# Batching TensorE's matmuls by tile shape in one cross-attention of a twelve-sublayer network

## Chip, core and metric

The kernel runs on one NeuronCore of a Trainium2 chip. The metric is the device time of one execution in microseconds, as a median of runs. All data are fp32. The engines named below are TensorE (PE in the profile, with its weight loads as PEld), VectorE (DVE), ScalarE (ACT), GpSimd (POOL) and SyncE (SP), which issues the DMAs.

## The reference, cut to what matters

The network has four layers, each with a cross-attention, a self-attention-like sublayer and a feed-forward one, over x of shape (64, 32, 128). The change is in the second layer's cross-attention, the fourth of twelve sublayers that run one after the other:

```python
x = x + _L1_xattn_ref(_layernorm(x), ctx_1024, ctx_1024, Wq, bq, Wk, bk, Wv, bv, Wo, bo)
# 16 heads of 64, 64 batches, 32 queries, 257 keys, ctx of shape (64, 257, 128)
scores = einsum('bhqd,bhkd->bhqk', q, k) / sqrt(64)
probs = softmax(scores, axis=-1)
z = einsum('bhqk,bhkd->bhqd', probs, v)          # then z @ Wo + bo
```

## The kernel before

Every sublayer is a function that writes the instruction streams of the engines by hand, with semaphores between them, and ends with a barrier of all engines. `l1_xattn` first folds the weights: `wqk[h]` is Wq times Wk of head h, `wvo[h]` is Wv times Wo, so keys and values are the raw context. Then `strip_attention` (tiles with the prefix `l1xs_`) works through 16 groups of 4 batches. A group has 16 heads; a head of a group is one step t, 256 steps in all.

For one group TensorE does four kinds of work, and they use three tile shapes of its array:

- `project(g, r)`, r = 0 to 3 (L2332): the queries of 4 heads, 4 matmuls of the full 128 by 128 array, into the bank `m_ps`. VectorE's `take_queries` (L2419) adds the bias and stores them in `qx`.
- `score(g, n)`, n = 0 to 15 (L2345): 4 matmuls on tiles of 128 rows by 32 columns, one for each batch, into one bank of 257 columns; the keys move.
- `weigh(g, j)`, j = 0 to 8 (L2357): 4 matmuls on tiles of 32 rows by 128 columns, for one strip of 32 keys of each batch, 512 columns each, into the four banks `u_ps`. ScalarE's `take_u` (L2401) copies the four banks to `ub`.
- `merge(g, heads)` (L2369): 16 matmuls of the full array with `wvo`, summed in `m_ps` as well. VectorE's `result` (L2442) adds the sum to X.

An fp32 matmul shows as two MATMUL records in the trace, so a score, a weighing or a quarter projection is 8 records and a merge 32.

Between score and weighing a step passes through the softmax: `maximum` on VectorE (L2425), `exp` on ScalarE with the sum of the row (L2393), `inverse` on VectorE (L2430), a scaling on GpSimd (L2467, tile `p`), and `turn` on VectorE, a transpose in 32 by 32 blocks (L2437, tile `pt`). `p` and `col` have four buffers. The scores have three banks, `s_ps`, used in turn: score t waits for exp of t - 3.

The order on TensorE is written out: in iteration i, after score n of group i + 1, it does a half merge of group i - 1 (n = 0, 1), a weighing of group i (n in `weigh_at`) or a quarter projection of group i + 2 (n in `project_at`). So almost every score is followed by work of another shape. On VectorE the order is also written out: step t does the maximum of t, the inverse of t - 1 and the turn of t - 2. ScalarE puts the four copies of `take_u` behind the exps 13, 14 and 15 of the next group. SyncE loads keys and values of each group two groups ahead into double buffers.

Of the kernel before, what the change touches and what calls it, by code (L numbers as in the profile page):

```python
# [11 lines left out]
ALU = mybir.AluOpType  # L12
ACT = mybir.ActivationFunctionType
AX = mybir.AxisListType
# [4 lines left out]
S2 = 257  # L19
KC, NKC = 86, 3  # L20
SP2 = KC * NKC
H = 16
# [3 lines left out]
GROUPS, STRIP = B // 4, 9  # L26
# [2264 lines left out]
def strip_attention(k, nm, wqk, bqk, wvo, bo, ph):  # L2291

    nc = k.nc
    s = {n: k.sem(nm + n) for n in ("q_mm", "qx", "s_mm", "mx", "exp", "rec", "norm", "pt", "u_mm", "u", "o_mm", "x",
                                    "pad")}
# [10 lines left out]
    weigh_at, project_at = (2, 3, 4, 6, 7, 8, 10, 11, 12), (5, 9, 13, 15)  # L2306

    with nc.Block() as block:
        @block.sync
# [11 lines left out]
        @block.tensor  # L2321
        def _(pe):
            def project(g, r):

                if r > 0:
                    pe.wait_ge(s["qx"], 4 * g + r)
                elif g > 0:
                    pe.wait_ge(s["qx"], 4 * g)
                    if g >= 3:
                        pe.wait_ge(s["x"], g - 2)  # L2330
                for h in range(4):
                    mm = nc.tensor.matmul(m_ps[:, h * 128:(h + 1) * 128], wqk[:, 4 * r + h, :], k.XN[:, cols(g)],  # L2332
                                          start=True, stop=True)
                mm.then_inc(s["q_mm"], 1)

            def score(g, n):
                t = 16 * g + n
                if n == 0:
                    pe.wait_ge(keys_in[g % 2], (g // 2 + 1) * 16)
                if n % 4 == 0:  # L2340
                    pe.wait_ge(s["qx"], 4 * g + n // 4 + 1)
                if t >= 3:
                    pe.wait_ge(s["exp"], t - 2)
                for c in range(4):
                    mm = nc.tensor.matmul(s_ps[t % 3][32 * c:32 * c + 32, :S2], qx[:, g % 2, n, 32 * c:32 * c + 32],  # L2345
                                          keys[:, g % 2, c, :S2], start=True, stop=True)
                mm.then_inc(s["s_mm"], 1)

            def weigh(g, j):
                if j == 0:  # L2350
                    pe.wait_ge(s["pt"], 16 * g + 16)
                    pe.wait_ge(vals_in[g % 2], (g // 2 + 1) * 16)
                    if g > 0:
                        pe.wait_ge(s["u"], 4 * g)
                for c in range(4):
                    r = slice(32 * c, 32 * c + 32)
                    mm = nc.tensor.matmul(u_ps[c][:], vals[r, g % 2, j, :], pt[r, g % 2, :, j, :], start=(j == 0),  # L2357
                                          stop=(j == STRIP - 1))
                if j == STRIP - 1:
                    mm.then_inc(s["u_mm"], 1)  # L2360

            def merge(g, heads):
                if heads[0] == 0:
                    pe.wait_ge(s["u"], 4 * g + 4)
                    pe.wait_ge(s["qx"], 4 * min(g + 3, GROUPS))
                    if g > 0:
                        pe.wait_ge(s["x"], g)
                for h in heads:
                    mm = nc.tensor.matmul(m_ps[:, :128], wvo[:, h, :], ub[:, :, h, :], start=(h == 0), stop=(h == H - 1))  # L2369
                if heads[-1] == H - 1:  # L2370
                    mm.then_inc(s["o_mm"], 1)

            for r in range(4):
                project(0, r)
            for i in range(-1, GROUPS + 1):
                for n in range(16):
                    if i + 1 < GROUPS:
                        score(i + 1, n)
                    if n < 2 and i >= 1:
                        merge(i - 1, range(8 * n, 8 * n + 8))  # L2380
                    if n in weigh_at and 0 <= i < GROUPS:
                        weigh(i, weigh_at.index(n))
                    if n in project_at and i + 2 < GROUPS:
                        project(i + 2, project_at.index(n))

        @block.scalar
        def _(act):
            def exp(g, n):
                t = 16 * g + n
# [3 lines left out]
                nc.scalar.activation(p[:, t % 4, :S2], s_ps[t % 3][:, :S2], ACT.Exp, bias=col[:, 0, t % 4:t % 4 + 1],  # L2393
                                     accum_out=col[:, 1, t % 4:t % 4 + 1]).then_inc(s["exp"], 1)

            def take_u(g, c):
                if c == 0:
                    act.wait_ge(s["u_mm"], g + 1)
                    if g > 0:
                        act.wait_ge(s["o_mm"], g)  # L2400
                nc.scalar.copy(ub[:, c].rearrange("p h q -> p (h q)"), u_ps[c][:]).then_inc(s["u"], 1)  # L2401

            act.wait_ge(s["pad"], 1)
            for i in range(-1, GROUPS):
                for n in range(16):
                    if i + 1 < GROUPS:
                        exp(i + 1, n)
                    if n >= 13 and i >= 0:
                        take_u(i, n - 13)
                if i >= 0:  # L2410
                    take_u(i, 3)

        @block.vector
        def _(dve):
            def take_queries(g, r):
                dve.wait_ge(s["q_mm"], 4 * g + r + 1)
                if g >= 2:
                    dve.wait_ge(s["s_mm"], 16 * (g - 2) + 4 * r + 4)
                nc.vector.tensor_tensor(qx[:, g % 2, 4 * r:4 * r + 4, :], m_ps.rearrange("p (h t) -> p h t", h=4),  # L2419
                                        bqk[:, 4 * r:4 * r + 4].unsqueeze(2).to_broadcast([128, 4, 128]), ALU.add  # L2420
                                        ).then_inc(s["qx"], 1)

            def maximum(t):
                dve.wait_ge(s["s_mm"], t + 1)
                nc.vector.tensor_reduce(col[:, 0, t % 4:t % 4 + 1], s_ps[t % 3][:, :S2], AX.X, ALU.max, negate=True  # L2425
                                        ).then_inc(s["mx"], 1)
# [12 lines left out]
            def result(g):  # L2439
                dve.wait_ge(s["o_mm"], g + 1)  # L2440
                x = k.X[:, cols(g)]
                nc.vector.scalar_tensor_tensor(out=x, in0=m_ps[:, :128], scalar=bo, in1=x, op0=ALU.add, op1=ALU.add  # L2442
                                               ).then_inc(s["x"], 1)
# [4 lines left out]
            last = 16 * GROUPS  # L2448
            for t in range(last + 2):
                if t < last:  # L2450
                    maximum(t)
                if 1 <= t <= last:
                    inverse(t - 1)
                if t >= 2:
                    turn(t - 2)
                if t % 16 == 2 and t // 16 >= 2:
                    result(t // 16 - 2)
                if t % 16 in project_at and t // 16 + 1 < GROUPS:
                    take_queries(t // 16 + 1, project_at.index(t % 16))
            result(GROUPS - 2)  # L2460
            result(GROUPS - 1)

        @block.gpsimd
# [1255 lines left out]
```

## Time and profile before

| | us |
|---|---|
| median of 3 runs | 3266.33 (3265.39 to 3274.02) |
| profiled execution, first to last instruction | 3273.0 |
| steps of the cross-attention in it, first score to last result | 509 to 962 |
| one group in its steady part | 28.0 |

The profiled execution has no time of its own beside its span; the span lies inside the spread of the three runs, so what surrounds the instructions is not seen as a separate term. The span is read as the time of that execution. A window of the trace is given in microseconds from the start of the span. A row of the timeline gives start, duration, engine, line, operation, tiles, shape and count.

### The profile page before, as it was taken

What the parts mean: (1) busy time and instruction counts of PE and PEld (TensorE: products, weight loads), DVE (VectorE), ACT (ScalarE), POOL (GpSimd) and SP (SyncE); (2) the same over time, 40 slices, a digit from 0 to 9 for tenths busy, and PEclk for the clock granted to TensorE, in tenths of its full rate; (3) what the DMA queues carried; (4) which work ended last, traced back from release to release, by engine and by line L of the source; (5) the groups of instructions that cost most, each with busy time, mean ns of one, the idle gap of its engine ahead of it and who ended that gap; (6) DMA issues with size and microseconds to landing.
All of it is one profiled execution on the core that took longest, in us unless ns stands there. A gap on an engine that the chain in (4) does not pass through costs nothing. (4 is left out here: it accounts for less than half of the span.)

```text
span 3273.0 us, 114088 instructions
## 1 busy us (share of the span) xinstructions
PE 2717.9 (83%) x49115; PEld 1960.9 (60%) x49115; DVE 2148.9 (66%) x5489; ACT 1435.8 (44%) x3330; POOL 571.5 (17%) x592
## 2 busy tenths in 40 slices
PE   8987478999986788888888887679999998697745
PEld 5645365444445576676767676557776666386633
DVE  3348335555547988898888888267777665664741
ACT  4343233333343354444544454357776434363410
POOL 0000334555550000000000000000001332161024
PEclk9879688999997899999999898979999998898865
DMA  2100331111110000000000000001111001252013
GB/s 81 53 18 14 101 122 49 43 43 43 43 57 3 3 4 4 4 5 4 4 4 4 4 4 4 3 20 26 26 26 44 1 1 34 82 133 68 5 44 106
DMA packets 69907, 109.22 MB, mean 33 GB/s; under 512 B 10336, under 2 KB 55024, under 8 KB 68880
## 3 DMA queue, kind: packets, MB, share of 16 engines
q1 hardware_dynamic: 57776, 80.34, 8.0%
q0 software_dynamic: 11696, 22.40, 2.7%
q8 instruction: 357, 5.85, 0.7%
q14 instruction: 78, 0.64, 0.1%
HBM read 90.06 MB, written 16.51 MB: 33 GB/s over the span
## 5 line engine op out<-in xcount | busy, mean ns | idle before, releaser
L3087 PE MATMUL psum<-l1d_rw,l1d_cols 64*32 64x32 f32 (+2 forms) x20480 | 238.9, 215 | 86.4 <-issue 65.9
L3087 PEld LDWEIGHTS psum<-l1d_rw,l1d_cols 64*32 64x32 f32 x20480 | 208.9, 107 | 131.0 <-issue 104.9
L2467 POOL TENSOR_SCALAR l1xs_p<-l1xs_p,l1xs_col 128x257 f32<-128x257 f32 x256 | 237.9, 932 | 243.8 <-DVE l1xs_col L2430 243.3
L2393 ACT ACTIVATE l1xs_p<-psum,l1xs_col 128x257 f32<-128x257 f32 x256 | 122.1, 477 | 258.7 <-DVE l1xs_col L2425 257.9
L2425 DVE TENSOR_REDUCE l1xs_col<-psum 128x1 f32<-128x257 f32 x256 | 107.1, 418 | 155.9 <-PE psum L2345 155.8
L1747 POOL TENSOR_SCALAR X<-X,l1f_bias 128x512 f32<-128x512 f32 x4 | 6.3, 1584 | 1140.5 <-DMA l1f_bias<-in_l1f_bias 1140.5
L3345 DVE TENSOR_TENSOR l1d_rw<-l1d_rw,l1d_tots 128x1536 f32<-128x1536 f32 x96 | 143.2, 1492 | 72.8 <-PE psum L3087 71.7
L2861 ACT COPY l1d_ya<-psum 128x512 f32<-128x512 f32 x160 | 92.8, 590 | 200.7 <-PE psum L3127 199.7
L2357 PE MATMUL psum<-l1xs_pt,l1xs_vals 32*128 32x512 f32 x1152 | 162.0, 637 | 1.9 <-DVE l1xs_pt L2437 1.9
L2345 PE MATMUL psum<-l1xs_keys,l1xs_qx 128*32 128x257 f32 x2048 | 160.8, 397 | 2.1 <-ACT l1xs_p L2393 2.1
L2683 ACT ACTIVATE l2x_p<-psum,l2x_top 128x257 f32<-128x257 f32 x256 | 120.5, 474 | 58.3 <-PE psum L2596 46.1
L3024 PE MATMUL psum<-l1d_src,l1d_wp 128*128 128x128 f32 x1024 | 138.2, 291 | 2.7 <-issue 1.3
L3024 PEld LDWEIGHTS psum<-l1d_src,l1d_wp 128*128 128x128 f32 x1024 | 127.7, 203 | 7.2 <-issue 3.7
L2437 DVE STREAM_TRANSPOSE l1xs_pt<-l1xs_p 128x288 f32<-128x288 f32 x256 | 118.0, 461 | 8.6 <-POOL l1xs_p L2467 8.1
L2596 PE MATMUL psum<-consts,l2x_p 128*86 128x128 f32 x768 | 120.6, 280 | 1.7 <-ACT l2x_p L2683 1.1
L2725 DVE TENSOR_REDUCE l2x_top<-psum 128x1 f32<-128x257 f32 x256 | 96.9, 420 | 36.6 <-PE psum L2585 32.9
L2345 PEld LDWEIGHTS psum<-l1xs_keys,l1xs_qx 128*32 128x32 f32 x2048 | 43.8, 109 | 123.7 <-issue 102.6
L1991 POOL TENSOR_TENSOR l2a_phi<-l2a_pos,l2a_ex 128x512 f32<-128x512 f32 x64 | 80.0, 1272 | 177.8 <-ACT l2a_ex L1977 177.8
L2596 PEld LDWEIGHTS psum<-consts,l2x_p 128*86 128x86 f32 x768 | 78.8, 122 | 33.5 <-issue 23.2
L3077 PE MATMUL psum<-l1d_small,l1d_hsel 32*128 32x384 f32 x256 | 65.5, 659 | 38.1 <-DVE l1d_small L3299 28.3
L2581 PE MATMUL psum<-l2x_keys,l2x_qx 32*128 32x257 f32 x512 | 90.1, 432 | 3.4 <-DMA l2x_mask<-l2x_table 3.4
L199 PE MATMUL psum<-consts,ln_xn 128*128 128x128 f32 x192 | 45.3, 397 | 50.5 <-ACT ln_xn L214 50.5
(558 smaller groups left out, 6926.6 us busy)
## 6 DMA issues: line engine op xcount, KB each, us to landing
l2f_w<-in_l2f_w SPq DMA_DIRECT2D x16, 768.0 KB
l1xs_vals<-in_ctx_strips SPq DMA_DIRECT2D x16, 576.0 KB
l0x_ctxT<-in_ctxT SPq DMA_DIRECT2D x16, 516.0 KB, 3.7
l1xs_keys<-in_ctxT SPq DMA_DIRECT2D x16, 516.0 KB
l2x_ctxT<-in_ctxT SPq DMA_DIRECT2D x64, 129.0 KB, 2.1
l1d_wp<-in_l1d_wp SPq DMA_DIRECT2D x1, 2048.0 KB, 7.9
l2f_acc<-l2f_zero SPq DMA_DIRECT2D x8, 256.0 KB, 3.6
l2f_sums<-l2f_acc SPq DMA_DIRECT2D x8, 256.0 KB, 3.4
```

Source lines behind the costliest of these rows:

```text
L2345: mm = nc.tensor.matmul(s_ps[t % 3][32 * c:32 * c + 32, :S2], qx[:, g % 2, n, 32 * c:32 * c + 32], keys[:, g % 2, c, :S2], start=True, sto ...
L2357: mm = nc.tensor.matmul(u_ps[c][:], vals[r, g % 2, j, :], pt[r, g % 2, :, j, :], start=(j == 0), stop=(j == STRIP - 1))
L2393: nc.scalar.activation(p[:, t % 4, :S2], s_ps[t % 3][:, :S2], ACT.Exp, bias=col[:, 0, t % 4:t % 4 + 1], accum_out=col[:, 1, t % 4:t % 4 + ...
L2425: nc.vector.tensor_reduce(col[:, 0, t % 4:t % 4 + 1], s_ps[t % 3][:, :S2], AX.X, ALU.max, negate=True).then_inc(s["mx"], 1)
L2437: nc.vector.transpose(pt[:, g % 2, n].rearrange("p j r -> p (j r)"), p[:, t % 4, :]).then_inc(s["pt"], 1)
L2467: nc.gpsimd.tensor_scalar(p[:, t % 4, :S2], p[:, t % 4, :S2], col[:, 2, t % 4:t % 4 + 1], None, ALU.mult).then_inc(s["norm"], 1)
L2596: mm = nc.tensor.transpose(t_ps[j % 2][:KC, c * 128:(c + 1) * 128], p[:, j, c * KC:(c + 1) * KC], k.const("ident"))
L2683: nc.scalar.activation(p[:, j, :S2], s_ps[j][:, :S2], ACT.Exp, bias=top[:, l % 2, j:j + 1], accum_out=sums[:, l % 2, j:j + 1]).then_inc(s[ ...
L2725: nc.vector.tensor_reduce(top[:, l % 2, j:j + 1], s_ps[j][:, :S2], AX.X, ALU.max, negate=True).then_inc(s["mx"], 1)
L3024: mm = nc.tensor.matmul(k.ps[into + j][:, e * 128:(e + 1) * 128], wp[:, n, c:c + 128], src[:], start=True, stop=True)
L3087: mm = nc.tensor.matmul(k.ps[bank0 + pr + e // per * 2][b * T:b * T + T, e % per * w:(e % per + 1) * w], cols[rr, 2 * n, e * 128 + b * T:e ...
L3345: tt(x, x, over.to_broadcast([128, feats.stop - feats.start, 32 * (16 >> lv), m]), ALU.mult)
```

## The change

TensorE's order is regrouped. An iteration has four batches; each is 4 scores of group i + 1, then 3 weighings of group i (or, in batch 0, the whole merge of group i - 1), then a quarter projection of group i + 2. The banks are dealt out again: scores use four banks, `ps[(t + 1) % 4]`, so score t waits for exp of t - 4; the queries have `ps[0]`, which is also the score bank of every fourth step of a batch, and the merge has `ps[1]`, which is that of every first step. For that a projection waits for the exp of the fourth score of its own batch, the fourth score waits for `take_queries` of the projection before, the merge waits for the exp of the first score of its batch, and the first score of batch 1 waits for `result` of the merge.

VectorE's order is regrouped too: the maxima, inverses and turns of the four steps of a batch are all done before it goes on to `result` (batch 0) and `take_queries`, and the maxima of the next batch come after these. ScalarE does the 16 exps of a group and then the four copies. GpSimd and SyncE keep their code.

```diff
-    s_ps, m_ps, u_ps = k.ps[0:3], k.ps[3], k.ps[4:8]
+    u_ps, query_ps, merge_ps = k.ps[4:8], k.ps[0], k.ps[1]
+    score_ps = lambda t: k.ps[(t + 1) % 4]
...
-                if r > 0:
-                    pe.wait_ge(s["qx"], 4 * g + r)
+                if g == 0 and r > 0:
+                    pe.wait_ge(s["qx"], r)
                 elif g > 0:
-                    pe.wait_ge(s["qx"], 4 * g)
-                    if g >= 3:
-                        pe.wait_ge(s["x"], g - 2)
+                    pe.wait_ge(s["exp"], 16 * (g - 1) + 4 * r + 4)
...
-                if t >= 3:
-                    pe.wait_ge(s["exp"], t - 2)
+                if t >= 4:
+                    pe.wait_ge(s["exp"], t - 3)
+                if n == 4 and g >= 2:
+                    pe.wait_ge(s["x"], g - 1)
+                if n == 3:
+                    pe.wait_ge(s["qx"], 4 * g + 4)
+                elif n % 4 == 3 and g + 1 < GROUPS:
+                    pe.wait_ge(s["qx"], 4 * (g + 1) + n // 4)
...
+            def merge(g):
+                pe.wait_ge(s["u"], 4 * g + 4)
+                pe.wait_ge(s["exp"], min(16 * (g + 2) + 1, 16 * GROUPS))
+                if g > 0:
+                    pe.wait_ge(s["x"], g)
+                for h in range(H):
...
             for i in range(-1, GROUPS + 1):
-                for n in range(16):
+                for batch in range(4):
                     if i + 1 < GROUPS:
-                        score(i + 1, n)
-                    if n < 2 and i >= 1:
-                        merge(i - 1, range(8 * n, 8 * n + 8))
-                    if n in weigh_at and 0 <= i < GROUPS:
-                        weigh(i, weigh_at.index(n))
-                    if n in project_at and i + 2 < GROUPS:
-                        project(i + 2, project_at.index(n))
+                        for n in range(4 * batch, 4 * batch + 4):
+                            score(i + 1, n)
+                    if batch == 0:
+                        if i >= 1:
+                            merge(i - 1)
+                    elif 0 <= i < GROUPS:
+                        for j in range(per * (batch - 1), per * batch):
+                            weigh(i, j)
+                    if i + 2 < GROUPS:
+                        project(i + 2, batch)
...
+            for g in range(GROUPS + 1):
+                if g < GROUPS:
+                    for t in range(16 * g, 16 * g + 16):
+                        exp(t)
+                if g > 0:
+                    take_u(g - 1)
...
+            for g in range(GROUPS):
+                for batch in range(4):
+                    t = 16 * g + 4 * batch
                     maximum(t)
+                    maximum(t + 1)
+                    inverse(t)
+                    maximum(t + 2)
+                    inverse(t + 1)
+                    maximum(t + 3)
+                    inverse(t + 2)
+                    turn(t)
+                    inverse(t + 3)
+                    turn(t + 1)
+                    turn(t + 2)
+                    turn(t + 3)
+                    if batch == 0 and g >= 2:
+                        result(g - 2)
+                    if g + 1 < GROUPS:
+                        take_queries(g + 1, batch)
```

## Rows read from the trace of the kernel before

**Rows 1.** The page's head.

```profile
span 3273.0 us, 114088 instructions
```

**Rows 2.** Windows: stretch, length, busy time of each engine, granted clock, DMA.

```profile
522.00:531.00 9.00, 5.71 (x72) 3.18 (x64) 7.87 (x27) 4.52 (x16) 6.91 (x9) 1.00 0.21 60
600.00:650.00 50.00, 48.09 (x476) 23.84 (x472) 29.41 (x95) 19.46 (x64) 26.36 (x29) 1.00 0.15 46
```

**Rows 3.** Waits from 560 to 900: total us, times, longest.

```profile
ACT l1xs_p L2393 <- DVE l1xs_col L2425: 209.0, 171, 2.6
...
PE psum L2369 <- ACT l1xs_ub L2401: 11.5, 12, 1.0
```

**Rows 4.** Timeline, one score and one weighing in mid-group.

```profile
700.13 0.64 PE L2345 MATMUL psum<-l1xs_keys,l1xs_qx 128*32 128x257 f32 x8
...
700.70 1.14 PE L2357 MATMUL psum<-l1xs_pt,l1xs_vals 32*128 32x512 f32 x8
700.84 0.43 DVE L2425 TENSOR_REDUCE l1xs_col<-psum 128x1 f32<-128x257 f32 x1 [0.54 <-PE psum L2345]
...
701.77 0.64 PE L2345 MATMUL psum<-l1xs_keys,l1xs_qx 128*32 128x257 f32 x8
```

**Rows 5.** Timeline, the passage from one group to the next.

```profile
719.25 1.16 PE L2332 MATMUL psum<-XN,l1x_wqk 128*128 128x128 f32 x8
...
720.34 0.64 PE L2345 MATMUL psum<-l1xs_keys,l1xs_qx 128*32 128x257 f32 x8
...
720.91 0.65 DVE L2419 TENSOR_TENSOR l1xs_qx<-psum,l1x_bqk 128x512 f32<-128x512 f32 x1
721.49 0.41 DVE L2425 TENSOR_REDUCE l1xs_col<-psum 128x1 f32<-128x257 f32 x1
...
721.93 0.48 ACT L2393 ACTIVATE l1xs_p<-psum,l1xs_col 128x257 f32<-128x257 f32 x1
...
721.93 2.05 PE L2369 MATMUL psum<-l1xs_ub,l1x_wvo 128*128 128x128 f32 x16 [0.96 <-ACT l1xs_ub L2401]
...
723.91 0.64 PE L2345 MATMUL psum<-l1xs_keys,l1xs_qx 128*32 128x257 f32 x8
```

**Rows 6.** Timeline, the first halves of the merges of groups 0, 13, 14.

```profile
554.07 2.05 PE L2369 MATMUL psum<-l1xs_ub,l1x_wvo 128*128 128x128 f32 x16 [0.96 <-ACT l1xs_ub L2401]
...
917.78 2.05 PE L2369 MATMUL psum<-l1xs_ub,l1x_wvo 128*128 128x128 f32 x16 [0.96 <-ACT l1xs_ub L2401]
...
942.62 5.47 PE L2369 MATMUL psum<-l1xs_ub,l1x_wvo 128*128 128x128 f32 x32 [3.16 <-ACT l1xs_ub L2401]
```

**Rows 7.** Timeline, the end: work of one shape in a row.

```profile
937.95 1.51 PE L2345 MATMUL psum<-l1xs_keys,l1xs_qx 128*32 128x257 f32 x24
...
948.02 8.01 PE L2357 MATMUL psum<-l1xs_pt,l1xs_vals 32*128 32x512 f32 x72
...
956.09 2.05 ACT L2401 COPY l1xs_ub<-psum 128x512 f32<-128x512 f32 x4 [13.52 <-PE psum L2357]
958.20 3.84 PE L2369 MATMUL psum<-l1xs_ub,l1x_wvo 128*128 128x128 f32 x32 [2.17 <-ACT l1xs_ub L2401]
```

**Rows 8.** Timeline, the first steps, where GpSimd works without a pause.

```profile
512.10 0.48 ACT L2393 ACTIVATE l1xs_p<-psum,l1xs_col 128x257 f32<-128x257 f32 x1
...
512.70 0.16 DVE L2430 RECIPROCAL l1xs_col<-l1xs_col 128x1 f32<-128x1 f32 x1 [1.12 <-ACT l1xs_p L2393]
...
512.97 4.78 POOL L2467 TENSOR_SCALAR l1xs_p<-l1xs_p,l1xs_col 128x257 f32<-128x257 f32 x5 [51.66 <-DVE l1xs_col L2430]
...
513.95 0.48 DVE L2437 STREAM_TRANSPOSE l1xs_pt<-l1xs_p 128x288 f32<-128x288 f32 x1 [0.62 <-POOL l1xs_p L2467]
...
516.77 0.48 DVE L2437 STREAM_TRANSPOSE l1xs_pt<-l1xs_p 128x288 f32<-128x288 f32 x1
...
517.18 0.65 DVE L2419 TENSOR_TENSOR l1xs_qx<-psum,l1x_bqk 128x512 f32<-128x512 f32 x1
```

**Rows 9.** A line's instructions: duration min, median, max in ns.

```profile
L2345 PEld LDWEIGHTS psum<-l1xs_keys,l1xs_qx x2048: 106/109/178, 509.1 to 938.9; 128*32 128x32 f32 x187
```

More of the change, by code:

```diff
@@ L2303, in strip_attention @@
     col = k.sb(nm + "col", [128, 3, 4], ctx=ph)
-    s_ps, m_ps, u_ps = k.ps[0:3], k.ps[3], k.ps[4:8]
+    u_ps, query_ps, merge_ps = k.ps[4:8], k.ps[0], k.ps[1]
+    score_ps = lambda t: k.ps[(t + 1) % 4]
     cols = lambda g: slice(g * 128, g * 128 + 128)
-    weigh_at, project_at = (2, 3, 4, 6, 7, 8, 10, 11, 12), (5, 9, 13, 15)
+    per = STRIP // 3
     with nc.Block() as block:
@@ L2341, in score @@
                     pe.wait_ge(s["qx"], 4 * g + n // 4 + 1)
[L2342 to L2343 removed]
+                if t >= 4:
[6 more added lines that the diff above has]
+                    pe.wait_ge(s["qx"], 4 * (g + 1) + n // 4)
                 for c in range(4):
[L2345 removed]
+                    mm = nc.tensor.matmul(score_ps(t)[32 * c:32 * c + 32, :S2], qx[:, g % 2, n, 32 * c:32 * c + 32],
                                           keys[:, g % 2, c, :S2], start=True, stop=True)
@@ L2360, in weigh @@
                     mm.then_inc(s["u_mm"], 1)
[L2362 to L2371, printed above, removed]
+            def merge(g):
[4 more added lines that the diff above has]
+                for h in range(H):
+                    mm = nc.tensor.matmul(merge_ps[:, :128], wvo[:, h, :], ub[:, :, h, :], start=(h == 0), stop=(h == H - 1))
+                mm.then_inc(s["o_mm"], 1)
             for r in range(4):
@@ L2375, in _, with exp @@
             for i in range(-1, GROUPS + 1):
-                for n in range(16):
+                for batch in range(4):
                     if i + 1 < GROUPS:
-                        score(i + 1, n)
-                    if n < 2 and i >= 1:
-                        merge(i - 1, range(8 * n, 8 * n + 8))
-                    if n in weigh_at and 0 <= i < GROUPS:
-                        weigh(i, weigh_at.index(n))
-                    if n in project_at and i + 2 < GROUPS:
-                        project(i + 2, project_at.index(n))
+                        for n in range(4 * batch, 4 * batch + 4):
[8 more added lines that the diff above has]
+                        project(i + 2, batch)
         @block.scalar
         def _(act):
-            def exp(g, n):
-                t = 16 * g + n
+            def exp(t):
                 act.wait_ge(s["mx"], t + 1)
@@ L2392, in exp, with take_u @@
                     act.wait_ge(s["pt"], t - 3)
-                nc.scalar.activation(p[:, t % 4, :S2], s_ps[t % 3][:, :S2], ACT.Exp, bias=col[:, 0, t % 4:t % 4 + 1],
+                nc.scalar.activation(p[:, t % 4, :S2], score_ps(t)[:, :S2], ACT.Exp, bias=col[:, 0, t % 4:t % 4 + 1],
                                      accum_out=col[:, 1, t % 4:t % 4 + 1]).then_inc(s["exp"], 1)
[L2396 to L2401, printed above, removed]
-            act.wait_ge(s["pad"], 1)
[L2404 to L2411, printed above, removed]
+            def take_u(g):
+                act.wait_ge(s["u_mm"], g + 1)
+                if g > 0:
+                    act.wait_ge(s["o_mm"], g)
+                for c in range(4):
+                    nc.scalar.copy(ub[:, c].rearrange("p h q -> p (h q)"), u_ps[c][:]).then_inc(s["u"], 1)
+            act.wait_ge(s["pad"], 1)
+            for g in range(GROUPS + 1):
+                if g < GROUPS:
+                    for t in range(16 * g, 16 * g + 16):
+                        exp(t)
+                if g > 0:
+                    take_u(g - 1)
         @block.vector
@@ L2418, in take_queries @@
                     dve.wait_ge(s["s_mm"], 16 * (g - 2) + 4 * r + 4)
-                nc.vector.tensor_tensor(qx[:, g % 2, 4 * r:4 * r + 4, :], m_ps.rearrange("p (h t) -> p h t", h=4),
+                nc.vector.tensor_tensor(qx[:, g % 2, 4 * r:4 * r + 4, :], query_ps.rearrange("p (h t) -> p h t", h=4),
                                         bqk[:, 4 * r:4 * r + 4].unsqueeze(2).to_broadcast([128, 4, 128]), ALU.add
@@ L2424, in maximum @@
                 dve.wait_ge(s["s_mm"], t + 1)
-                nc.vector.tensor_reduce(col[:, 0, t % 4:t % 4 + 1], s_ps[t % 3][:, :S2], AX.X, ALU.max, negate=True
+                nc.vector.tensor_reduce(col[:, 0, t % 4:t % 4 + 1], score_ps(t)[:, :S2], AX.X, ALU.max, negate=True
                                         ).then_inc(s["mx"], 1)
@@ L2441, in result @@
                 x = k.X[:, cols(g)]
-                nc.vector.scalar_tensor_tensor(out=x, in0=m_ps[:, :128], scalar=bo, in1=x, op0=ALU.add, op1=ALU.add
+                nc.vector.scalar_tensor_tensor(out=x, in0=merge_ps[:, :128], scalar=bo, in1=x, op0=ALU.add, op1=ALU.add
                                                ).then_inc(s["x"], 1)
@@ L2447, in _ @@
                 take_queries(0, r)
-            last = 16 * GROUPS
-            for t in range(last + 2):
-                if t < last:
+            for g in range(GROUPS):
+                for batch in range(4):
+                    t = 16 * g + 4 * batch
                     maximum(t)
[L2452 to L2459, printed above, removed]
+                    maximum(t + 1)
[13 more added lines that the diff above has]
+                        take_queries(g + 1, batch)
             result(GROUPS - 2)
```

2 lines of the change are left out of this document (1 added, 1 removed).

## Prediction

> **What bounds the kernel now.** The head of the page gives the span, 3273.0 us [rows 1]; the median of the runs is 3266.33. The change touches one stretch, 509 to 962 us, and a barrier closes it, so what that stretch gains, the whole gains. I read the windows first: from 600 to 650 TensorE is busy for 48.09 of 50 us at the full clock (2.4 GHz), GpSimd for 26, VectorE for 29 [rows 2]. A full TensorE can still be wasting time at its seams, so the waits come next: ScalarE waits 209 us in all for the maxima, because these wait for scores, while TensorE has one wait of note, the merge for `take_u`, 12 times about 1 us [rows 3]. TensorE sets the pace.
>
> Then the timeline, start to start. Mid-group a score is followed by a weighing after 0.57 us, and that by a score after 1.07 [rows 4]. A quarter projection takes 1.09 up to the next score, a half merge 1.98, and the merge starts 1.59 after the score before it instead of 0.57, a stall of 1.02 [rows 5]. One group is 15 scores x 0.57 + 1 score before a score x 0.44 (below) + 9 weighings x 1.07 + 4 x 1.09 + 2 x 1.98 = 26.94, with the stall 27.96. The merges of groups 0 and 13 start 363.71 us apart, 13 groups of 27.98 [rows 6]. The sum closes.
>
> **What the same work costs in a row.** Three scores take 1.51 against 0.64 for one [rows 7, 4], so a score behind a score costs 0.435, not 0.57. Nine weighings take 8.01 [rows 7], one 1.14 [rows 4]: each further one 0.86, not 1.07. A merge in one piece takes 3.84 and a half one 2.05 [rows 7, 5]: 1.79 for 16 more records, 0.112 each. So leaving a shape costs 0.13 after a score, 0.21 after a weighing, about 0.2 after full-array work.
>
> **Part 1, TensorE's order.** A batch with weighings becomes 3 x 0.435 + 0.57 = 1.88 for the scores, 2 x 0.86 + 1.07 = 2.79 for the weighings, 1.09 for the projection: 5.76. Batch 0 has the merge, 32 x 0.112 = 3.58, followed by full-array work without a seam: 1.88 + 3.58 + 1.09 = 6.55. Four batches: 23.83 us, 3.1 less than 26.94, for 11 seams where there were 30. This is TensorE's need; whether it gets its work in time is part 2.
>
> A rule would deny this part. First the rows: the weights of a score are 8 loads of 109 ns [rows 9], and they don't show in 0.435 us, so they lie under the matmuls of the score before. The Trainium skill (TensorE: Matmul & The Clock Gate, Part 3, The mechanism) says that a weight load overlaps running matmuls only when it goes to another row group; scores use all rows. By it a score behind a score would cost 0.435 + 8 x 0.109 = 1.31 and a batch 2.6 us more. This trace disagrees, and the rows decide.
>
> **Part 2, VectorE's order, the new bound.** Until now the steps flowed through VectorE one by one. Now a batch goes in and out before the next maximum. Let D be the start of the first maximum of a batch. The exp starts 0.44 later (721.49 to 721.93) [rows 5]; the inverse 0.60 after it; GpSimd 0.27 after that; the first turn 0.98 after GpSimd's start; and the fourth turn 2.82 after the first, since GpSimd scales one step in 0.94; five in a row take 4.78, at most 0.96 each [rows 8]. That is D + 5.11. `take_queries` follows 0.41 later (516.77 to 517.18) [rows 8], at D + 5.52, and the next maximum 0.58 after it (720.91 to 721.49) [rows 5]: D + 6.10. The other three maxima and inverses fit into the gaps: with 0.4 a maximum the fourth is read at about D + 1.6 and its exp is over at D + 2.6, before GpSimd needs it at D + 4.1. So a batch takes 6.10 on VectorE against 5.76 on TensorE. VectorE and GpSimd in series become the bound by 0.34.
>
> TensorE's new waits under this pace: the projection (for the fourth exp, D + 2.6) comes after scores and weighings, about D + 4, so it is not held. The fourth score waits for `take_queries`, over 0.65 us after its start; the three scores before it fill that time. The fourth bank lets all four scores start before VectorE has left the batch before. These waits I cost at nothing; their cover is TensorE's slack of 0.34 per batch and the scores running ahead, and each 0.1 that a handover costs beyond it would add 0.4 per group.
>
> **Batch 0.** The merge may not start before the first exp of its batch, D + 1.04; counted from the `take_queries` before, at 0.58 + 1.04 = 1.62. Then 3.58 for the merge and 1.16 + 0.07 for the projection to be seen [rows 5]; the 0.07 is what lies between a score's end and its maximum [rows 4]: the next `take_queries` 6.43 after the last. VectorE with `result` (about 0.3, the size of a short read of a bank) would allow 6.4. So 6.43. The stall for `take_u` goes: the four copies take 2.05 [rows 7], start when the ninth weighing is over, about 1.8 before batch 0's pace begins, and are done before ScalarE owes the first exp. If `take_u` came 0.8 later, it would push that exp and with it the batch.
>
> One group: 6.43 + 3 x 6.10 = 24.73, against 27.98: 3.25 less, 13 times, **-42.2**.
>
> **The start.** Before, work of the first group flowed ahead of the first weighing. Now the whole pipe keeps to 6.10. The first `take_queries` of group 1 stands at 517.18 in either order, since the four turns before it hang on GpSimd; D follows at 517.76. Seven more batches without a merge give 517.76 + 42.70 = 560.46, and the first merge starts 1.04 later, 561.5, where it was 554.07 [rows 6]: **+7.4**.
>
> **The last scores.** From merge 13 to merge 14 were 24.84 us [rows 6]. Now VectorE has no `take_queries` there: batch 0 ends with `result` over at D + 5.83, the first score of batch 1 waits for it and is seen 0.71 later [rows 4], about D + 6.6; two more batches of 5.52 lead to D + 17.6; the last exp is over 2.6 later, the copies take 2.05, the handover 0.06: merge 14 at D + 22.4, or 21.3 after merge 13: **-3.5**. Behind that the same work remains (weighings, copies, merge, result), **0**; merge 14 ran partly at the lower clock, 5.47 against 3.84 [rows 6, 7], and may keep or lose these 1.6.
>
> DMAs: the same 32 loads with the same release rules, 0.15 of the queues [rows 2]; 0.
>
> **Sum.** -42.2 + 7.4 - 3.5 = **-38.3**. Span 3273.0 - 38.3 = 3234.7; against the median, 3266.3 - 38.3 = **3228**.
>
> **Unknown costs.** What isn't seen in rows is a batch of four under these waits. From below: VectorE's chain hides more than I think and TensorE binds at 23.83: 13 x 4.15 = 54 gained, start +5 (seven batches of 5.76), end -3.5: 3214. From above: each batch loses a handover of 0.07 twice more and the start runs at the half clock for a while; 63 batches x 0.14 = 9, and a few us for batches whose 3 us of TensorE work per 6 leave it idle, though it stayed at the full clock with 5.71 of 9 us busy [rows 2]: 3228 + 9 + 6 = 3243. I take the middle, since each link of the 6.10 has a row of the same pair of instructions.
>
> **Rivals.**
> 1. *TensorE stays the bound*, 3214. For it: 5.76 and 6.10 are close. Against: the chain through GpSimd has no link that the change shortens. 10%.
> 2. *Handovers add up*: every new wait costs, 6.3 to 6.5 a batch, 3240 to 3256. For it: four engines take turns within each batch, with little slack in batch 0. Against: before, these handovers cost 0.03 to 0.07. 12%.
> 3. *The seams are not of shape*: the 0.13 to 0.21 stay with each piece of work. Then TensorE needs 26.9 a group, 1.0 less than now; with start and end 3266 - 13 + 7 - 3 = 3257, no change. Against: rows 7. 3%.
> 4. *Slower by GpSimd*: the fourfold scaling lies bare in the chain of each batch. 0.1 us more on each scaling, by working beside the transposes all the time, is 0.4 a batch, 25 us in all. At 1.09 us (now 0.94) the gain is gone, at 1.13 it is slower by 0.3%; at 1.2 it would be 3292. Against: five in 4.78 beside VectorE's transposes. 2%.
> 5. *Slower by weight loads*, when a score's loads can't lie under the score before: TensorE 5.76 + 2.6 = 8.4 a batch, 34 a group, about 80 us slower, 3346. Against: the three scores in 1.51. 1%. It is the result of the skill's rule above.
>
> **How the numbers follow.** My own case has 72%, 3228 with 3220 to 3240 as its own range. The range 3212 to 3244 takes in rival 1 and the near part of rival 2. From no change a measurement of this kernel can tell about 0.3%, 9.8 us: faster is below 3256.5. Faster: 72 + 10 + 12 = 94, less 1 for the tail of rival 2, 93%; same: 4%; slower: 3%.
>
> **What the profile after would show.** Part 1: scores as records x32 in about 1.95 us, weighings x24 in some 2.9, merges in one piece. Part 2: merges about 24.7 us apart; `take_queries` 6.1 apart inside a group; GpSimd in runs of four, 4 x 0.94 long, with pauses of some 2.3; small waits of TensorE, below 0.5 us, for `take_queries` or the exp. The first merge near 561 to 562. I am wrong if GpSimd's runs are longer, if the copies of `take_u` stand in front of a first exp that VectorE is waiting for, or if TensorE's clock falls inside the groups.

## The result, and the profile after

The changed kernel takes 3231.34 us (median of 4 runs, 3211.16 to 3238.58) against 3267.39 for the kernel before: ratio 0.988, interval 0.9853 to 0.9907. A second comparison gave 3221.05 against 3263.69, ratio 0.9861 (0.9836 to 0.9886). Both intervals lie clear of 1, so the kernel is faster, by 1.2 and 1.4%; the prediction was 3228, faster. The profiled execution spans 3236.8 us and took 3238.58, so 1.8 us lie around the span.

The changed kernel's windows come first, with the columns of [rows 2]:

```profile
600.00:650.00 50.00, 49.39 (x544) 29.84 (x540) 35.80 (x110) 21.22 (x76) 30.32 (x34) 1.00 0.13 47
```

In the same 50 us TensorE now handles 544 matmul records where it were 476, at the same full clock: 14% more, with little more busy time. That fits fewer seams; the pairs below test it. The waits, from 570 to 860, as in [rows 3]:

```profile
ACT l1xs_p L2398 <- DVE l1xs_col L2428: 149.0, 47, 4.4
...
DVE l1xs_pt L2440 <- POOL l1xs_p L2477: 59.5, 143, 0.4
...
DVE l1xs_col L2433 <- ACT l1xs_p L2398: 21.4, 95, 0.3
...
PE psum L2373 <- issue: 2.9, 12, 0.2
```

VectorE waited for TensorE's scores before, in this row of the waits of the kernel before from 560 to 900:

```profile
DVE l1xs_col L2425 <- PE psum L2345: 130.2, 135, 2.3
```

Now it waits for GpSimd (143 turns) and ScalarE (95 inverses). TensorE's row for the merge has gone from 1 us each to 0.2. One group in the timeline (`take_u` is L2406 here, `take_queries` L2422, `merge` L2373):

```profile
699.87 2.06 ACT L2406 COPY l1xs_ub<-psum 128x512 f32<-128x512 f32 x4 [1.13 <-PE psum L2362]
...
701.55 0.65 DVE L2422 TENSOR_TENSOR l1xs_qx<-psum,l1x_bqk 128x512 f32<-128x512 f32 x1
...
703.24 3.81 PE L2373 MATMUL psum<-l1xs_ub,l1x_wvo 128*128 128x128 f32 x32 [0.24 <-issue]
...
707.98 0.69 DVE L2422 TENSOR_TENSOR l1xs_qx<-psum,l1x_bqk 128x512 f32<-128x512 f32 x1
707.98 1.94 PE L2350 MATMUL psum<-l1xs_keys,l1xs_qx 128*32 128x257 f32 x32
...
709.85 2.86 PE L2362 MATMUL psum<-l1xs_pt,l1xs_vals 32*128 32x512 f32 x24
...
712.64 1.16 PE L2331 MATMUL psum<-XN,l1x_wqk 128*128 128x128 f32 x8
...
714.09 0.65 DVE L2422 TENSOR_TENSOR l1xs_qx<-psum,l1x_bqk 128x512 f32<-128x512 f32 x1
714.67 0.74 DVE L2428 TENSOR_REDUCE l1xs_col<-psum 128x1 f32<-128x257 f32 x2
715.11 0.48 ACT L2398 ACTIVATE l1xs_p<-psum,l1xs_col 128x257 f32<-128x257 f32 x1 [3.83 <-DVE l1xs_col L2428]
...
715.71 0.16 DVE L2433 RECIPROCAL l1xs_col<-l1xs_col 128x1 f32<-128x1 f32 x1 [0.30 <-ACT l1xs_p L2398]
...
715.97 3.66 POOL L2477 TENSOR_SCALAR l1xs_p<-l1xs_p,l1xs_col 128x257 f32<-128x257 f32 x4 [2.31 <-DVE l1xs_col L2433]
...
716.93 0.48 DVE L2440 STREAM_TRANSPOSE l1xs_pt<-l1xs_p 128x288 f32<-128x288 f32 x1
...
719.66 0.48 DVE L2440 STREAM_TRANSPOSE l1xs_pt<-l1xs_p 128x288 f32<-128x288 f32 x1 [0.43 <-POOL l1xs_p L2477]
720.06 0.65 DVE L2422 TENSOR_TENSOR l1xs_qx<-psum,l1x_bqk 128x512 f32<-128x512 f32 x1
```

From `take_queries` to `take_queries`: batch 0 is 701.55 to 707.98 = 6.43, batch 1 up to 714.09 = 6.11, batch 2 up to 720.06 = 5.97, as is batch 3: 24.48. Within batch 2, from 714.09 to 720.06, every link of the chain can be read: 0.58, 0.44, 0.60, 0.26, 0.96, then 2.73 for three turns, then 0.40. The scores need 1.87 to the first weighing, the three weighings 2.79 to the projection, as the sum had it. The merges of groups 0, 13 and 14 stand at:

```profile
556.30 3.81 PE L2373 MATMUL psum<-l1xs_ub,l1x_wvo 128*128 128x128 f32 x32 [0.29 <-ACT l1xs_p L2398]
...
874.62 3.81 PE L2373 MATMUL psum<-l1xs_ub,l1x_wvo 128*128 128x128 f32 x32 [0.24 <-issue]
895.58 3.84 PE L2373 MATMUL psum<-l1xs_ub,l1x_wvo 128*128 128x128 f32 x32 [2.17 <-ACT l1xs_ub L2406]
```

318.32 / 13 = 24.49 us a group, where it was 27.98 [rows 6].

To compare the sublayer between executions I measure it from VectorE's fill of the padding of `p` (498.65 before, 494.33 after) to the first load of the next sublayer (963.31 and 914.63). It went from 464.7 to 420.3: 44.4 us less, while the span fell by 36.2. The other 8.2 us were lost in sublayers that are the same code in both; the experiments below return to them. The expectations of the first four runs below count to the start of the last `result` instead, 1.2 us less: their 419.1 is the 420.3 here.

### The profile page after: what moved, and what is told of

It reads as the page before. It is cut to its first block and busy times, and to the rows that moved or that the text cites. A ratio compares the mean times of both kernels' runs of the same rounds, so it can differ in the third digit from the quotient of the medians.

```text
span 3236.8 us, 114135 instructions
## 1 busy us (share of the span) xinstructions
PE 2687.6 (83%) x49115; PEld 1991.0 (62%) x49115; DVE 2164.4 (67%) x5489; ACT 1427.3 (44%) x3330; POOL 568.7 (18%) x592
## 5 line engine op out<-in xcount | busy, mean ns | idle before, releaser
L2350 PE MATMUL psum<-l1xs_keys,l1xs_qx 128*32 128x257 f32 x2048 | 134.3, 395 | 3.8 <-DVE l1xs_qx L2422 1.9
L2362 PE MATMUL psum<-l1xs_pt,l1xs_vals 32*128 32x512 f32 x1152 | 136.6, 604 | 0.0
L2350 PEld LDWEIGHTS psum<-l1xs_keys,l1xs_qx 128*32 128x32 f32 x2048 | 61.9, 112 | 54.6 <-issue 25.6
L2331 PEld LDWEIGHTS psum<-XN,l1x_wqk 128*128 128x128 f32 x512 | 66.1, 202 | 46.7 <-issue 32.6
```

What stands on the lines that cost most here:

```text
L2350: mm = nc.tensor.matmul(score_ps(t)[32 * c:32 * c + 32, :S2], qx[:, g % 2, n, 32 * c:32 * c + 32], keys[:, g % 2, c, :S2], start=True, sto ...
```

## The experiments

The sublayer's length is in the sense just given, a group's is from merge to merge over 12 or 13 groups, and the first merge is counted from the fill of the padding (before 55.4, after 62.0). "Others" is the span without the sublayer. The kernels of two weighings and of 128 columns leave out work and do not compute the function; they are here for their times alone. The kernel before took 3280.1 us in the one execution of its second profile.

| kernel | sublayer | group | first merge | others | time, ratio to before |
|---|---|---|---|---|---|
| before, two profiles | 464.7, 464.7 | 27.98 | 55.4 | 2808.3, 2813.5 | 3263.7 to 3268.1 |
| after, two profiles | 420.3, 421.8 | 24.49, 24.48 | 62.0 | 2816.5, 2799.6 | 3231.3; 3221.1, 0.986 |
| two weighings of three | 420.0 | 24.48 | 61.9 | 2799.0 | 3220.8 (1 run) |
| scaling of 128 columns | 404.8 | 23.77 | 54.5 | 2805.4 | 3212.0 (1 run) |
| flowing VectorE order | 413.1 | 23.77 | 62.8 | 2805.4 | 3214.6, 0.9835 |
| scores in pairs | 429.2 | 24.82 | 64.2 | 2791.4 | 3222.4 (1 run) |
| VectorE's order alone | 530.0 | 32.26 | 63.3 | 2809.3 | 3341.3 (1 run) |
| early maxima | 408.1 | 23.77 | 57.8 | 2793.6 | 3204.7, 0.9813 |

**What sets the 5.97 us of a batch?** Two kernels, one that takes work from TensorE and one that takes it from GpSimd.

```diff
                         for j in range(per * (batch - 1), per * batch):
-                            weigh(i, j)
+                            if j % 3 != 1:
+                                weigh(i, j)
```

> TensorE leaves out the middle weighing of each three (3 of the 9 strips of keys are not weighed), all else as in the changed kernel. Theory A (VectorE and GpSimd in series set the 5.97 us of a batch): batches 1 to 3 keep 5.97 us and a group 24.49; only the nine weighings of the last group lose 2.6 us, so the cross-attention takes about 416 us for 419.1. Theory B (TensorE sets the pace): each batch loses 0.86 us, a group 2.6, the cross-attention 35 to 39 us.

The merges of groups 0 and 12:

```profile
547.64 3.81 PE L2373 MATMUL psum<-l1xs_ub,l1x_wvo 128*128 128x128 f32 x32 [0.29 <-ACT l1xs_p L2399]
...
841.43 3.81 PE L2373 MATMUL psum<-l1xs_ub,l1x_wvo 128*128 128x128 f32 x32 [0.24 <-issue]
```

293.79 / 12 = 24.48. A ninth part of TensorE's time was taken out of each group and nothing came back (from 600 to 650 it is busy for 44.90 of 50 us): TensorE isn't the bound. The small gain expected at the end is missing too (420.0, not some 417): without the weighings TensorE stood idle for 4.57 us ahead of merge 14, which then ran mostly at the lower clock (1.2 GHz; the merge took 6.36 us for 3.84), and that ate the 2.6 saved behind it.

```diff
-nc.gpsimd.tensor_scalar(p[:, t % 4, :S2], p[:, t % 4, :S2], col[:, 2, t % 4:t % 4 + 1], None, ALU.mult
+nc.gpsimd.tensor_scalar(p[:, t % 4, :128], p[:, t % 4, :128], col[:, 2, t % 4:t % 4 + 1], None, ALU.mult
```

> GpSimd scales 128 of the 257 columns of each step (the others stay unscaled), all else as in the changed kernel. Theory A (chain through GpSimd): the four scalings shorten by about half, the chain falls below TensorE's own 5.76 us, so batches 1 to 3 take 5.76 and batch 0 about 6.55, a group 23.85; with the start, which is all chain, the cross-attention takes 400 to 406 us for 419.1. Theory B (TensorE or the handovers set the pace): a group stays within 0.2 of 24.49 and the cross-attention loses at most 3 us.

The scaling's durations (minimum, median, maximum in ns), then the merges of groups 0 and 13:

```profile
L2477 POOL TENSOR_SCALAR l1xs_p<-l1xs_p,l1xs_col x256: 596/605/621, 509.5 to 876.1; 128x128 f32<-128x128 f32 x128
549.64 3.83 PE L2373 MATMUL psum<-l1xs_ub,l1x_wvo 128*128 128x128 f32 x32
...
858.68 3.84 PE L2373 MATMUL psum<-l1xs_ub,l1x_wvo 128*128 128x128 f32 x32
```

309.04 / 13 = 23.77, and the start got 7.5 us shorter. With GpSimd's part cut TensorE is the bound, busy for all of 600 to 650, at 23.77 where I had summed 23.83. The two together settle it: the chain through VectorE, ScalarE and GpSimd sets the changed kernel's pace, 0.72 us a group above what TensorE needs.

**Which half of the change gains?** TensorE's batches with VectorE stepping as before:

```diff
-            for g in range(GROUPS):
-                for batch in range(4):
-                    t = 16 * g + 4 * batch
...
+            for t in range(last + 2):
+                if t < last:
+                    maximum(t)
+                if 1 <= t <= last:
+                    inverse(t - 1)
+                if t >= 2:
+                    turn(t - 2)
+                if t % 4 == 3:
+                    g, batch = divmod(t // 4, 4)
+                    if batch == 0 and g >= 2 and g < GROUPS:
+                        result(g - 2)
+                    if g + 1 < GROUPS:
+                        take_queries(g + 1, batch)
```

> TensorE, banks and ScalarE as in the changed kernel, but VectorE goes step by step as in the kernel before (maximum of t, inverse of t - 1, turn of t - 2), with the queries taken after the step that ends a batch. Theory A (seams are the gain, the batching of VectorE gives some of it back): TensorE binds, batches 5.76, batch 0 6.58, a group 23.86; first weighings come about 7 us earlier; the cross-attention takes about 403 us for 419.1, the whole some 15 us less than the changed kernel, ratio to the kernel before 0.982 to 0.986. Theory B (VectorE's new order is needed for TensorE to run in batches): a group takes 24.5 or more and the time is no better than that of the changed kernel.

3214.6 us (3200.0 to 3220.3), ratio 0.9835 (0.9807 to 0.9863). 23.77 a group, and TensorE is busy for all of this window:

```profile
600.00:650.00 50.00, 50.00 (x560) 30.72 (x556) 34.19 (x109) 24.42 (x78) 30.35 (x34) 1.00 0.15 50
```

So VectorE's new order isn't needed for TensorE's batches; it costs 0.72 a group. But the start did not come earlier, 62.8 for 62.0, where 7 us less was expected; the sublayer is 413.1 and not 404 (403 as the expectation counts). The timeline of a batch without weighings shows why:

```profile
524.55 0.42 DVE L2428 TENSOR_REDUCE l1xs_col<-psum 128x1 f32<-128x257 f32 x1
...
527.00 0.48 DVE L2440 STREAM_TRANSPOSE l1xs_pt<-l1xs_p 128x288 f32<-128x288 f32 x1
527.41 0.39 DVE L2428 TENSOR_REDUCE l1xs_col<-psum 128x1 f32<-128x257 f32 x1
...
528.45 1.16 PE L2331 MATMUL psum<-XN,l1x_wqk 128*128 128x128 f32 x8 [2.67 <-ACT l1xs_p L2398]
```

The fourth maximum (527.41) stands behind a turn that waits for GpSimd, 2.86 after the first (524.55). The projection waits for the exp of that step (2.67 us idle), and the next maxima wait for the projection: 5.7 us a batch. I had taken the fourth maximum at D + 1.6, which holds only for the batched order. A second part is the clock. Behind the next idle stretch of 2.67 us the granted clock fell to the lower level (1.2 GHz) for a while: a projection took 1.91 us for 1.16 and the four scores of the first batch with weighings 2.80 for 1.94, so that two `take_queries` stand 6.60 apart there, where the later batches with weighings have 5.75. Batches before it ran partly at that level too.

```profile
534.14 1.91 PE L2331 MATMUL psum<-XN,l1x_wqk 128*128 128x128 f32 x8 [2.67 <-ACT l1xs_p L2398]
...
535.99 2.80 PE L2350 MATMUL psum<-l1xs_keys,l1xs_qx 128*32 128x257 f32 x32
```

The other half alone, VectorE's batches in the kernel before (its TensorE order, its three score banks):

> The kernel before with only VectorE's order changed to batches of four steps (three score banks, TensorE and ScalarE as before). Theory A (that part of the change brings nothing and costs something): TensorE keeps its 30 seams, so a group takes at least 28.0 us, and with VectorE leaving each batch before the next and only three banks 28 to 31; the cross-attention 465 to 510 us. Theory B (batches on VectorE are a gain of their own): a group under 27.5.

The waits from 590 to 900:

```profile
ACT l1xs_p L2393 <- DVE l1xs_col L2425: 206.1, 68, 4.5
POOL l1xs_p L2474 <- DVE l1xs_col L2430: 170.5, 58, 6.0
DVE l1xs_col L2425 <- PE psum L2345: 64.1, 30, 4.0
```

3341.3 us; 32.26 a group, above even the 31 that I had given as the most, and a sublayer of 530.0, above the 510. VectorE must have seen all four maxima before it turns the first step, while TensorE delivers scores 1.64 apart, so each batch waits for its last score and then drains through GpSimd. TensorE pays at two places in each group:

```profile
622.44 2.02 PE L2369 MATMUL psum<-l1xs_ub,l1x_wvo 128*128 128x128 f32 x16 [2.78 <-issue]
...
680.46 0.64 PE L2345 MATMUL psum<-l1xs_keys,l1xs_qx 128*32 128x257 f32 x8 [1.14 <-ACT l1xs_p L2393]
...
684.78 0.65 DVE L2419 TENSOR_TENSOR l1xs_qx<-psum,l1x_bqk 128x512 f32<-128x512 f32 x1
...
685.53 3.14 PE L2369 MATMUL psum<-l1xs_ub,l1x_wvo 128*128 128x128 f32 x16 [2.77 <-issue]
```

The merge idles for 2.8 us, where it was 1.0: it shares its bank with the queries, and `take_queries` (684.78) now stands behind all four turns of its batch. One score idles for 1.1, for an exp that frees its bank. Two groups in the windows:

```profile
589.35:622.44 33.09, 28.93 (x264) 13.97 (x265) 17.98 (x54) 10.44 (x36) 14.66 (x16) 0.95 0.12 36
622.44:653.99 31.55, 27.38 (x265) 12.94 (x265) 17.99 (x54) 10.44 (x36) 14.65 (x16) 1.00 0.12 36
```

At the full clock a group takes 31.55, 3.6 more than before, of which these idle times are some 3.2 (2.8 + 1.1 and three short ones of 0.1, less the 1.0 of before). Six of the 13 groups take 33.1: behind the idle stretch the granted clock fell to the lower level (1.2 GHz) for a while, and the group lost 1.55; over the 13 groups that is the other 0.7 of the 4.3. VectorE's order is worth something only with scores that come in batches.

**Are the seams the gain?** On the flowing order, where TensorE is the bound, the same matmuls with two seams more in each batch:

```diff
-                    if i + 1 < GROUPS:
-                        for n in range(4 * batch, 4 * batch + 4):
+                    for n in range(4 * batch, 4 * batch + 4):
+                        if i + 1 < GROUPS:
                             score(i + 1, n)
+                        if n % 4 == 1 and batch > 0 and 0 <= i < GROUPS:
+                            weigh(i, per * (batch - 1))
...
-                        for j in range(per * (batch - 1), per * batch):
+                        for j in range(per * (batch - 1) + 1, per * batch):
                             weigh(i, j)
```

> On top of the flowing VectorE order, where TensorE sets the pace with 23.77 us a group, the four scores of batches 1 to 3 stand in two pairs with one weighing between them: the same matmuls with two seams more in each batch. Theory A (leaving a shape costs 0.13 us after a score and 0.21 after a weighing): 0.34 a batch, 1.0 a group, 24.8; the cross-attention takes 427 to 428 us for 413.2. Theory B (the gain came from the waits and banks, not from the seams): a group stays within 0.2 of 23.77.

```profile
643.15 1.07 PE L2350 MATMUL psum<-l1xs_keys,l1xs_qx 128*32 128x257 f32 x16
644.16 1.14 PE L2362 MATMUL psum<-l1xs_pt,l1xs_vals 32*128 32x512 f32 x8
645.23 1.07 PE L2350 MATMUL psum<-l1xs_keys,l1xs_qx 128*32 128x257 f32 x16
646.23 2.00 PE L2362 MATMUL psum<-l1xs_pt,l1xs_vals 32*128 32x512 f32 x16
648.16 1.16 PE L2331 MATMUL psum<-XN,l1x_wqk 128*128 128x128 f32 x8
```

643.15 to 648.16 is 5.01 us for four scores and three weighings; with the four scores in a row and the three weighings in a row it is 1.87 + 2.79 = 4.66. 0.35 for two seams, three times a group 1.05: 23.77 + 1.05 = 24.82, what was measured. The matmuls and VectorE's order are the same, and TensorE is busy for all of 600 to 650 in both. The sublayer, 429.2, is 16.1 above that of the flowing order, a little more than the 14 to 15 expected: the 13 groups are 13.7 of it, the stretch from merge 13 to merge 14 is 1.05, and the first merge comes 1.4 later.

**The 8 us outside.** The changed kernel and the kernel before, each once more:

> The changed kernel once more, unchanged, for the parts of the program that the change does not touch. Theory A (the cross-attention gained more than the whole, the rest is chance of TensorE's clock in other sublayers): the cross-attention, from the fill of the padding of p to the last result, takes 419.1 us again within 0.5, a group 24.49, while the other sublayers differ by several us between runs at different granted clocks; the times spread over some 20 us. Theory B (the change makes later sublayers slower, by where it leaves the clock or the loads): the sublayers behind take the same 12 us more than in the kernel before again.

> The kernel before, unchanged, for the sublayers that the change does not touch. Theory A (chance): one of them takes other times than in the first profile by up to 10 us, the last cross-attention between 99 and 107 us and its granted clock moves with it; the changed cross-attention takes 464.7 us again. Theory B (the change slows the last cross-attention): 99 us again here, against 103 to 107 in every profile of a changed kernel.

The column of the others answers: 2791 to 2817 over ten profiles, the kernel before 2808 and 2814, the changed one 2817 and 2800. So the untouched code isn't slower in the changed kernel as a rule. The largest single difference of the first pair, the last cross-attention (99.3 us before, 105.7 after), in windows of the kernel before, first profile:

```profile
2981.80:3081.10 99.30, 81.08 (x1294) 62.91 (x1294) 70.90 (x153) 44.48 (x78) 0.00 (x0) 0.79 0.08 27
```

of the kernel before, second profile:

```profile
2988.40:3091.00 102.60, 84.64 (x1294) 65.62 (x1294) 70.92 (x153) 44.56 (x78) 0.00 (x0) 0.75 0.07 26
```

and of the changed kernel:

```profile
2937.50:3043.20 105.70, 86.69 (x1294) 66.24 (x1294) 71.10 (x153) 44.20 (x79) 0.00 (x0) 0.73 0.08 25
```

The same 1294 matmul records, granted clocks of 0.79, 0.75 and 0.73: the length follows the clock. Against the first window TensorE's busy time grows by 3.6 and 5.6 us, and the length by 3.3 and 6.4. The kernel before takes these 3.3 us more the second time, where theory B wanted 99 again. Of the 8.2 us of the first pair this stretch has 6.4; the rest I didn't take apart. Its 102.6 lies just under the 102.8 to 106.8 of the other eight profiles; two profiles of the kernel before are too few to exclude a small effect. The changed kernel's sublayer itself varies by the clock too: 421.8 in its second profile, 1.5 more where at most 0.5 was expected, because merge 14 took 5.47 there and 3.84 in the first.

**A version that is faster than the kernel before and the changed one.** It keeps the maxima early, as in the changed kernel, and puts the last two turns of a batch into the gaps of the next one, as the flowing order does. The edit against the changed kernel:

```diff
+            last = 16 * GROUPS
             for g in range(GROUPS):
                 for batch in range(4):
...
                     maximum(t)
                     maximum(t + 1)
+                    if t > 0:
+                        turn(t - 2)
                     inverse(t)
                     maximum(t + 2)
+                    if t > 0:
+                        turn(t - 1)
                     inverse(t + 1)
                     maximum(t + 3)
                     inverse(t + 2)
+                    inverse(t + 3)
                     turn(t)
-                    inverse(t + 3)
                     turn(t + 1)
-                    turn(t + 2)
-                    turn(t + 3)
                     if batch == 0 and g >= 2:
                         result(g - 2)
                     if g + 1 < GROUPS:
                         take_queries(g + 1, batch)
+            turn(last - 2)
+            turn(last - 1)
```

> TensorE in batches; VectorE takes the maxima of a batch early and puts the last two turns of a batch behind the first maxima of the next one. Theory A (the first batches, which have no weighings, are a chain from the first maximum over the fourth exp to the projection; with the fourth maximum early this chain is 4.5 us and not 5.7): a group 23.8 as with the flowing order, the first merge 6 to 7 us earlier, the cross-attention 406 to 409 us for 413.2 and 420.3, ratio to the kernel before 0.980 to 0.984. Theory B (the start hangs on the clock, half rate while TensorE has little to do, or on GpSimd): the first merge moves by less than 2 us.

3204.68 us (3200.59 to 3207.96) against 3268.11: ratio 0.9813 (0.9791 to 0.9835), below the intervals of both comparisons of the changed kernel, if narrowly for the second. Against the flowing order the whole times don't decide (its interval overlaps), the sublayer does: 408.1 for 413.1. A group keeps 23.77 and the first merge comes at 57.8, 5.0 earlier than with the flowing order. The first projections:

```profile
510.44 1.16 PE L2331 MATMUL psum<-XN,l1x_wqk 128*128 128x128 f32 x8 [1.79 <-ACT l1xs_p L2398]
...
515.25 1.16 PE L2331 MATMUL psum<-XN,l1x_wqk 128*128 128x128 f32 x8 [1.78 <-ACT l1xs_p L2398]
...
521.16 3.63 PE L2350 MATMUL psum<-l1xs_keys,l1xs_qx 128*32 128x257 f32 x32
525.93 1.16 PE L2331 MATMUL psum<-XN,l1x_wqk 128*128 128x128 f32 x8 [1.15 <-ACT l1xs_p L2398]
```

4.81 a batch, not 5.7 and not the 4.5 expected, and one batch whose scores ran at the lower clock (3.63 for 1.94) takes 5.9. So the explanation of the missing start holds, 0.89 a batch where both kernels run at the full clock, but it isn't the whole: 0.85 of the 5.0 is the batch with weighings that the flowing order ran partly at the lower clock, and the clock has a share in the other batches too, which I can't separate. The mean granted clock up to the first merge was 0.83 here and 0.81 there.

## Why the prediction was right

The forecast by its own steps, each against the first profile after:

| step | predicted | measured |
|---|---|---|
| TensorE's need for a group | 23.83 | 23.77 (where it binds) |
| batch 0 | 6.43 | 6.43 |
| batch 1 | 6.10 | 6.11 |
| batches 2 and 3 | 6.10 | 5.97 |
| a group | 24.73 | 24.49 |
| 13 groups | -42.2 | -45.4 |
| start | +7.4 | +6.5 |
| last scores | -3.5 | -3.9 |
| behind them | 0 | -1.6 (0 in the second profile) |
| sublayer | -38.3 | -44.4 |
| other sublayers | 0 | +8.2 (-13.9 in the second profiles) |
| span | -38.3 | -36.2 |

**Part 1** was right and is shown: where TensorE binds, a group takes 23.77, and the pairs of scores give back 0.35 for two seams, 0.34 predicted. That a score behind a score shows no weight load is seen again: 32 records in 1.94 us. The Trainium skill's rule in TensorE: Matmul & The Clock Gate, Part 3, The mechanism, by which a batch would take 2.6 us more, does not hold in this trace either. The prediction took one sentence of that section; another sentence of the same section of the Trainium skill also lets a load run ahead when it goes to the background weight buffer, so the section as a whole doesn't force those 2.6 us. No run here tells which way the loads take, only that they don't show.

**Part 2** was right in mechanism: the chain through GpSimd took over as the bound. It was mis-sized by 0.13 in batches 2 and 3. Of this 0.09 is the term of the four scalings: the fourth turn follows the first after 2.73, not 2.82; the other 0.04 are three links that came out 0.01 to 0.02 shorter. GpSimd isn't faster in the changed kernel: a scaling takes 0.93 us in both, and scalings that don't wait start 0.91 to 0.93 apart in both. The prediction read 0.94 as GpSimd's own pace, but the five scalings of [rows 8] start 0.93, 1.00, 0.91 and 1.00 apart: twice GpSimd idled for 0.07, because the inverse it needed was late. The flowing order puts a maximum behind a turn that waits for GpSimd (513.95), and the inverse behind that:

```profile
514.35 0.39 DVE L2425 TENSOR_REDUCE l1xs_col<-psum 128x1 f32<-128x257 f32 x1
...
514.66 0.14 DVE L2430 RECIPROCAL l1xs_col<-l1xs_col 128x1 f32<-128x1 f32 x1
```

With this inverse over at 514.80 the third scaling starts at 514.90. The batched order has the inverses early and four scalings in 3.66; the flowing order on the new TensorE order has one such pause in each batch and takes 3.75; the early maxima, with maxima between the turns but no late inverse, take 3.65. 2 x 0.13 x 13 = 3.4 are the 3.2 us that the 13 groups gained beyond the forecast, within rounding. The start has the same term: `take_queries` come 5.97 apart there too, 7 x 0.13 = 0.9 less than forecast, which is +6.5 for +7.4, though the mean granted clock up to the first merge was 0.80 (0.84 before). Batch 1 has the shorter chain too but gives it back: its first score starts only at 707.98, when `result` has freed the bank and the projection is over, so the first maximum comes 0.70 after `take_queries` and not 0.58.

**Batch 0**: the wait of the merge for the first exp, 1.62 after `take_queries`, is measured as 703.24 - 701.55 = 1.69, and `take_u` was over in time, at 701.93, before the first exp of the batch at 702.57.

**The sum** of the span was nearer than its terms, and that is luck: the sublayer gained 6.1 us more than forecast, and 8.2 were lost in other code, 6.4 of them in the stretch whose length follows the clock. 1.6 of the 6.1 are luck as well: in the first profile merges 14 and 15 both ran at the full clock, while in the second, and in eight of the ten in all, one of the two took 5.5. The sublayer gained 44.4 between the first profiles and 42.9 between the second ones, and the medians fell by 36.1 and 42.6 in the two comparisons; the forecast of 38.3 for the sublayer was some 5 to 6 us short. In the fourth rival one figure is 1 us low: 0.26 more on each of 252 scalings is 65.5, so 3293 and not 3292.

**The rivals**: TensorE as the bound is refuted by the left out weighings; handovers that add up by the 6.43 and 5.97; seams that aren't of shape by the pairs; GpSimd slower beside the transposes by its starts 0.91 apart; weight loads by the 1.94. The mechanism of the fourth rival is real all the same: with GpSimd's part cut by a third the sublayer gained 15.5 us, in one run.

## What to carry to other kernels

Where TensorE is the bound and alternates between tile shapes, count the seams and price them start to start in the trace: alike matmuls behind alike ones against the mixed pair. When one engine's order is batched, draw the chain of a batch through all the others, from the first read of the bank to the last release, before copying the batching to them, and ask whether a duration read from rows holds a wait of the old order: here the other engines had to take the batch's start early but didn't have to finish it before the next. Compare the touched stretch between two profiles, since the untouched rest of a long program can move by as much as the effect.

## What the runs showed of the hardware

- A change of TensorE's tile shape costs 0.35 us for the pair of a change after 128 by 32 scores and one after 32 by 128 weighings, at the full clock (5.01 against 4.66 us for the same seven pieces of work). The start-to-start times split it: 0.57 for 0.435 us, so 0.13 after a score, and 1.07 for 0.86, so 0.21 after a weighing.
- GpSimd's scaling of 128 by 257 fp32 values takes 0.93 us and that of 128 by 128 0.605: half the columns save 35%. An estimate from the two, if the cost grows in proportion to the columns: some 0.28 of each is fixed. Without a wait they start 0.91 to 0.93 apart, with VectorE's transposes alone or with maxima beside them (3.66 us for four beside transposes, 3.65 with maxima between).
- TensorE's granted clock fell to the lower level (1.2 GHz) after idle stretches even in this dense sublayer, and not always after the same one: merge 14 took 3.84 and 5.47 us in two profiles of the same kernel after 2.17 us of idling, and 6.36 after 4.57. With VectorE's order alone TensorE idled for 2.8 us ahead of each merge; in 6 of 13 groups the clock then fell for a while and the group took 1.55 us more, in the others it stayed.
